# GpSimd's row transfers moved between the result transfers, in a routed-expert kernel

## The reference

```
x = x + _layernorm(_L0_attn_ref(_layernorm(x, axis=-1), W_in, W_gate, b_gate, rms_w, W_out), axis=-1)
x = x + _layernorm(_L0_ffn_ref(_layernorm(x, axis=-1), router_weight, router_bias, ...), axis=-1)

_L0_attn_ref:  gates = (x @ W_in.T) @ W_gate.T + b_gate; then along the sequence
    c = f * c + i * cd
    c_norm = c * jax.lax.rsqrt(jnp.mean(c * c, axis=-1, keepdims=True) + EPS) * rms_w
    h = o * jnp.tanh(c_norm)

_L0_ffn_ref:
    logits = x @ router_weight.T + router_bias
    top_val, top_idx = jax.lax.top_k(logits, TOP_K)
    top_val = jax.nn.softmax(top_val, axis=-1)
    gate_up = jnp.einsum('th,ehd->etd', x, gate_up_proj) + gate_up_proj_bias[:, None, :]
    glu = gate * jax.nn.sigmoid(gate * ALPHA)
    out = jnp.einsum('etd,edh->eth', (up + 1.0) * glu, down_proj) + down_proj_bias[:, None, :]
    out = out * router_scores.T[:, :, None]
    out = out.sum(axis=0)
```

## Time and profile before

| what | value |
|---|---|
| median of 3 runs | 755.52 us (750.88, 755.52, 762.74) |
| the profiled execution's own time | 761.46 us |
| its span, from the first to the last instruction | 759.3 us |
| mean granted clock of PE | 0.893 of full speed |
| share of the span that PE, DVE, ACT, POOL are busy | 85%, 68%, 61%, 51% |
| row transfers on POOL ahead of the result transfers (L987) | 112 |
| row transfers between them (L1008) | 16 |
| result transfers (L1019) | 143 |

### The profile page before, as it was taken

The page is one execution under the profiler, slowest core; times in us unless marked ns, Lnnn a source line. Parts: engine busy times, 40 slices in busy tenths (PEclk is TensorE's granted clock), DMA queues, the critical chain, the costliest instruction groups (busy, mean ns, idle before and its releaser), DMA issues.

```text
span 759.3 us, 13499 instructions
## 1 busy us (share of the span) xinstructions
PE 646.2 (85%) x3800; PEld 418.5 (55%) x3800; DVE 518.0 (68%) x1478; ACT 460.1 (61%) x929; POOL 389.8 (51%) x299
## 2 busy tenths in 40 slices
PE   5888998798999955578999999999999999987460
PEld 2344656364756644434666666666666666654240
DVE  3626487758788887846767777777777777760892
ACT  2687796637485554335776777777777767761242
POOL 0001223333576677667777756666666666664121
PEclk9999899969899966589999999999999999995555
DMA  7966862789532332646788775677776776755997
GB/s 242 420 274 106 170 113 38 185 301 345 177 121 95 114 114 93 183 138 114 153 187 174 121 105 94 104 118 107 113 113 108 118 111 107 105 59 84 347 171 109
DMA packets 111207, 114.86 MB, mean 151 GB/s; under 512 B 31426, under 2 KB 100818, under 8 KB 109474
## 3 DMA queue, kind: packets, MB, share of 16 engines
q0 software_dynamic: 35312, 50.22, 38.8%
q1 hardware_dynamic: 75826, 63.79, 28.2%
HBM read 54.94 MB, written 59.03 MB: 150 GB/s over the span
## 4 chain that ended last, share of the span: by engine, by line
PE 62%; DVE 15%; DMA 7%; ACT 6%; issue 5%; SPq 2%; POOL 1%; another core or an unknown queue 0%; POOLq 0%; ACTq 0%; DVEq 0%
PE PS L672 8%; PE PS L671 8%; PE PS L670 8%; PE PS L521 7%; PE PS L690 4%; PE PS L659 4%; PE PS L691 4%; PE PS L692 4%; PE PS L678 4%; PE PS L554 3%; PE PS L546 3%; DMA W<-w_dn 2%; PE PS L574 2%; DMA W<-neg_mem 2%; PE PS L562 2%
## 5 line engine op out<-in xcount | busy, mean ns | idle before, releaser
L1019 POOL DMA_INDIRECT sums<-arena x143 | 222.0, 1552 | 114.0 <-DMA sums<-arena 52.5
L987 POOL DMA_INDIRECT routed<-arena,small x112 | 121.3, 1083 | 87.1 <-DMA routed<-arena,small 71.3
L1405 DVE TENSOR_SCALAR arena<-PS,small 128x256 f32<-128x256 f32 x143 | 77.8, 544 | 96.8 <-ACT arena L944 71.6
L521 PE MATMUL PS<-arena 128*128 128x512 f32 x256 | 126.9, 637 | 8.0 <-ACT arena L744 5.8
L944 ACT ACTIVATE arena<-PS,small 128x256 f32<-128x256 f32 x143 | 67.7, 474 | 102.6 <-PE PS L672 89.6
L744 ACT ACTIVATE arena<-PS 128x512 f16<-128x512 f16 (+1 forms) x179 | 104.5, 590 | 33.9 <-PE PS L499 11.7
L670 PE MATMUL PS<-W,arena 128*128 x286 | 109.9, 384 | 0.2 <-issue 0.2
L672 PE MATMUL PS<-W,arena 128*128 x286 | 109.8, 384 | 0.0
L671 PE MATMUL PS<-W,arena 128*128 x286 | 109.7, 383 | 0.0
L690 PE MATMUL PS<-W,arena 128*128 x286 | 78.6, 275 | 6.3 <-DVE arena L1395 3.2
L521 PEld LDWEIGHTS PS<-arena 128*128 128x128 f32 x256 | 49.6, 205 | 58.7 <-issue 53.9
(11 more groups left out here) (181 smaller groups left out, 1053.9 us busy)
## 6 DMA issues: line engine op xcount, KB each, us to landing
arena<-routed SPq DMA_DIRECT2D x143, 128.0 KB
W<-w_gu SPq DMA_DIRECT2D x8, 1024.0 KB, 23.4
W<-neg_mem POOLq DMA_DIRECT2D x16, 512.0 KB
sums<-zero SPq DMA_DIRECT2D x2, 4096.0 KB
W<-sums SPq DMA_DIRECT2D x16, 512.0 KB, 8.8
X<-x SPq DMA_DIRECT2D x8, 512.0 KB, 4.7
W<-w_dn SPq DMA_DIRECT2D x4, 1024.0 KB, 11.3
out<-X SPq DMA_DIRECT2D x8, 512.0 KB
```

The lines of the kernel that those rows point to most:

```text
L521: last = mm(PS[:, 2 + c % 2, :], WcT[:, k, c * P:(c + 1) * P], xT[:, k, :], start=(k == 0), stop=(k == KT - 1))
L987: pool.indirect_dma_start(routed, bass.IndirectOffsetOnAxis(ap=idx, axis=0), rows[b][:, jk // TOPK, :], None).then_inc(rows_sent[lane], 16)
L1019: pool.indirect_dma_start(sums[j % SUMS], bass.IndirectOffsetOnAxis(ap=dst[j % MU], axis=0), yb[u], None, compute_op=ALU.add).then_inc(y_s ...
L1405: L.send(v.tensor_scalar(up[j % 2], acc[:, FF:2 * FF], gu_hi, gu_lo, ALU.min, ALU.max))
```

## The change

`EARLY` goes from 48 to 64, and the new constant `AHEAD` is 8. POOL now sends all rows of blocks 0 to 5 and the first 8 of block 6 ahead of the result transfers (104 for 112). The other 8 of block 6 and the 16 of block 7 stand one behind each second tile, behind tiles 1, 3, ..., 47 (24 for 16). The first table covers 64 tiles and is still made from the counts of blocks 0 to 4; the second covers 79 for 95. SP's wait for all row transfers goes from ahead of tile 48 to ahead of tile 64. PE's two-bank order with its wait holds for tiles up to 63.

```
-EARLY = 48
+EARLY = 64
+AHEAD = 8
...
                 pool.wait_ge(slot_ready, t + 1)
                 pool.wait_ge(lo_ready, t + 1)
-                for jk in range(BT * TOPK):
+                for jk in range(BT * TOPK if t < NBLK - 2 else AHEAD):
...
-            def last_row(jk):
-                t = NBLK - 1
+            def late_row(n):
+                t, jk = divmod(BT * TOPK * (NBLK - 2) + AHEAD + n, BT * TOPK)
                 if jk == 0:
                     pool.wait_ge(slot_ready, t + 1)
                     pool.wait_ge(lo_ready, t + 1)
...
-                if j % 2 and j // 2 < BT * TOPK:
-                    last_row(j // 2)
+                if j % 2 and j // 2 < 2 * BT * TOPK - AHEAD:
+                    late_row(j // 2)
```

## The result

The change takes 752.06 us (median of 21 runs, 748.42 to 766.09) where the kernel before takes 756.48 us (median of 21, 750.88 to 765.48). The ratio is 0.9932, with a 95% interval of 0.9912 to 0.9951: 5.1 us faster, and beyond the noise. The ratio and its interval leave out the executions of each kernel that ran in a slower state, so the ratio is not quite that of the medians. The forecast was 758 us.

A forecast was written before the change was run, and what follows sets the result against it. The prediction took POOL's list of result transfers as the bound: 0 for the head start plus 2.4 us for eight row transfers, a ratio of 1.003 on the 755.52 us median, gave 758 us, range 747 to 768 us.

The forecast's parts named there:

- What bounds the kernel: End of the tile stage: POOL's list of result transfers, waiting for landings, sets it, 12.2 us behind the last copy.
- The rest of the change: Table, two-bank order and SP's later wait: no cost; 9 us of lead left at tile 64, PE does not wait.
- The head start: POOL's first result transfer: could come at about 335.3 instead of 340.42, but the gain is lost by tile 7: 0 us.
- the gain at tile 7: POOL's transfer of tile 7: POOL waited 2.43 us for ACT there, so arriving earlier changes nothing.
- The price: POOL's list, tiles 32 to 47: eight more row transfers between results at 0.3 us each, +2.4 us.
- The difference of the paces: POOL's result transfers with row transfers between them against those without: 0.42 us a row transfer, 3.4 us for eight.
- the stretch with a hole in it: POOL from 427.88 to 477.10, 2.59 us an interval with a 3.72 us hole: 0.11 us a row transfer, the lower bound.
- The faster rival: PE in tiles 5 to 7: results come 6.9 us earlier without the dense row transfers; sum -4.5 us, 751 us, chance 0.28.
- The prediction's sign for this rival: POOL's tile 7 transfer: if it comes well before 359.88, the faster rival holds.
- The slower rival: POOL's list, tiles 32 to 47: each added row transfer costs its whole 1.31 us, +10.5 us, 766 us, chance 0.15.
- The delay paid back: POOL's chain catches up with PE by the end, so neither price nor early gain shows: 755.5 us, chance 0.12.
- PE's three steps: PE's row transposes from tile 5 to tile 8: 14.16 us for three tiles where its pace is 2.41 us, 6.9 us lost.

The follow-up runs named there:

- Half results: The change with each result transfer sending 128 of the 256 numbers of each row, 64 KB for 128 KB: 742.66 us, ratio 0.9791 to the kernel before.
- AHEAD = 4: The change with AHEAD 4 for 8, so four of block 6's row transfers ahead and 28 between results: 763.43 us, ratio 1.0052 to the kernel before.
- The table alone: The change with AHEAD = 16, all block 6 rows ahead of results again, first table still 64 tiles: 757.54 us, ratio 0.9991 to the kernel before.
- the second trace of the kernel before: The kernel before, run again without an edit for another trace: 760.38 us, one run.
- the added ones: The change with 16 more row transfers, behind each second result transfer of tiles 49 to 79: 765.71 us, ratio 1.0075 to the kernel before.
- the two traces of the change: The change's profiled execution, 766.09 us, and one from running it again without an edit: 756.10 us, ratio 0.9936 to the kernel before.
- the first transfer held: The change with POOL's first result transfer also waiting for the result copy of tile 4: 764.97 us, ratio 1.008 to the kernel before.

## Why the prediction was wrong

**What bounds the kernel: right.** The landings of result transfers end the tile stage, behind a PE that is no slower than they are. Half results show it. In the traces with whole results POOL is 10.7 to 19.8 us behind the last copy, but for the kernel with AHEAD = 4, where PE itself stood still.

**The rest of the change: right.** The table alone is worth 0.9991. Counted from the first row copy, SP loaded tile 64 at 150.2 us where 157.6 was estimated, PE did not wait there, and ACT's result copies come 2.44 us apart from tile 32 to 47 and 2.41 us from there to tile 137. (The 2.47 us a tile that the second window above seems to give is too long, as PE's last gate and up matmul comes 6 us before its end; in the kernel before that is 4 us, so the 2.42 us of the prediction is slightly long too, and the copies say 2.41.)

**The head start: here it failed.** The step reads "With the same times of PE's results, the gain at tile 7 is nothing". It took the times of results from one execution, in which PE had lost 6.9 us in tiles 5 to 7. In the second trace of the kernel before, PE loses half a microsecond there, POOL is 13.1 us behind ACT's copy at the first tile and still 9.5 us at tile 13. Between the two kernels the gain at tile 13 is 57.0 to 57.5 against 48.8 to 49.1, some 8 us. In its place the runs showed a head start that is kept. The wait of 2.43 us ahead of tile 7's transfer was true of that execution, but the change does not have those same times of results.

**The price: somewhat too low.** I took 0.3 us a row transfer, 2.4 us. It is 0.66 us by the added ones (0.4 to 0.9), 5.3 us for eight, and 0.37 to 0.58 us by the traces. The difference of the paces, 0.42 us, was the better choice; leaning towards the stretch with a hole in it was the mistake. 8 us of head start less 3 to 5 us is 3 to 5 us, and 5 us were measured. At tile 47, with nearly all row transfers sent, the two traces of the change are 5.0 us ahead of the two of the kernel before on average.

**The faster rival: near in size, wrong in cause.** It gave 751 us, for a PE freed of the dense row transfers. But beside the same dense row transfers PE takes 7.74 us for the three tiles in the second trace and 8.28 us with the table alone, where the change takes 7.42. Those 0.3 to 0.9 us may be theirs, though the kernel with the first transfer held takes 8.03 us without them; the 6.9 us did not come again with them. The prediction's sign for this rival, an early transfer of tile 7, could not tell it from a head start that is kept: that transfer stands at 41.2 us in the second trace of the kernel before too, without the long steps.

**The slower rival** did not happen at 1.31 us each, though the price went half the way to it. **The delay paid back** did not happen either, by the ratios: the first transfer held by 10 us cost 10.9 us.

**What stays open.** Why PE's three steps took 14.16 us in that one execution; the nine other traces have 7.3 to 8.3 us, so it could not be tried. A part of it is the clock: PE's granted clock was 0.78 of full speed from 335 to 340 and 0.88 from 340 to 345 there. Whether the price is over 0.42 us, and if so why: that the added transfers delay the landings of results was not measured by itself. And how the delay of the first transfer held reaches the end, as its one trace has most of it gone by tile 142.

## What to carry to other kernels

Where two engines run at the same pace, a late start may never be made up, so look for what delays its first item and not only for what lengthens each one. Before a forecast builds on a wait of a few microseconds that happened once, ask whether the change alters whose wait it is, and whether another execution has it: a stretch hidden behind a late engine costs next to nothing and tells nothing of what freeing that engine is worth. Work moved behind a later item also moves every wait for its landing: keep the distance between them, or the next engine pays for it at once.

## What the runs showed of the hardware

An accumulating indirect DMA of 128 rows took 3.8 us to land with 1 KB a row (the median of 143 in the second trace of the kernel before; those in the chains that ended last took 3.46 to 5.64 us), and 3.4 us with 512 bytes (the median with half results). An indirect DMA of 128 rows of 1152 bytes kept POOL busy for 0.97 to 1.01 us, and between two waiting result transfers about half of its 1.31 us shows in the end (0.66 us, uncertain between 0.4 and 0.9).
